# A graph layer on one core: two norms staggered in the last stage, one joint gather, and weights loaded during other stages

## What is computed

```python
K = typed_linear(x, Wk, bk, node_type)      # out[i] = x[i] @ W[type of i] + b[type of i]
Q = typed_linear(x, Wq, bq, node_type)
V = typed_linear(x, Wv, bv, node_type)
...                                         # attention over the edges, both ways; agg: [6250, 256]
h = jnp.concatenate([agg, agg], axis=1)
o = typed_linear(h, Wa, ba, node_type)      # Wa: [19, 512, 256]
y = o + x
mu = y.mean(axis=-1, keepdims=True)
var = y.var(axis=-1, keepdims=True)
yn = (y - mu) / jnp.sqrt(var + LN_EPS)
r = yn * gamma[node_type] + beta[node_type]
x = _layernorm(x + r, axis=-1)              # a second norm, over the sum with x
```

## Time and profile before

| | us |
|---|---|
| median of 3 runs (10157.53 to 10163.48) | 10160.39 |
| the profiled execution | 10144.25 |
| its span in the trace | 10142.5 |
| `project`: first load to PE's first product stage | 95.3 to 147.2 |
| `store_sums` and the loads of `output`: to PE's first transpose | 9388 to 9462.9 |
| the 18 turns of `output` and what follows them | 9462.9 to 10142.5 |

### The profile page before, as it was taken

How to read it: one execution, slowest core, us unless ns; L and a number is a source line. 1 busy time by engine, 2 the same in 40 slices (tenths; PEclk the granted TensorE clock), 3 DMA queues, 4 the chain that set the end, 5 groups by cost and what they waited for, 6 DMA issues and landing times. The chain is left out here.

```text
span 10142.5 us, 138050 instructions
## 1 busy us (share of the span) xinstructions
PE 6538.8 (64%) x34160; PEld 4384.0 (43%) x34161; DVE 6599.2 (65%) x13813; ACT 4385.9 (43%) x13293; POOL 5739.0 (57%) x5509
## 2 busy tenths in 40 slices
PE   3778666666664677777777677613666374998455
PEld 1257444444442444444444444402555263776222
DVE  1059999999996666666666666642555277888223
ACT  0100444444442555555555555412555274887111
POOL 3230677777776677777777777757888400000232
PEclk5665555555555888888888888756989797999555
DMA  2110000000001788888888888858999985887210
GB/s 67 46 53 0 9 9 9 9 9 9 9 9 42 246 262 262 261 260 261 258 260 260 258 260 260 230 182 272 336 332 336 194 199 166 258 259 225 94 35 12
DMA packets 1345184, 1653.53 MB, mean 163 GB/s; under 512 B 419468, under 2 KB 1144951, under 8 KB 1344777
## 3 DMA queue, kind: packets, MB, share of 16 engines
q1 hardware_dynamic: 868170, 967.89, 29.8%
q0 software_dynamic: 261440, 671.33, 22.0%
q10 hardware_dynamic: 215424, 12.91, 2.5%
HBM read 1047.72 MB, written 635.41 MB: 166 GB/s over the span
## 5 line engine op out<-in xcount | busy, mean ns | idle before, releaser
L1109 PE MATMUL exch_pG<-exch_tab,exch_ohT 128*128 x3328 | 1555.8, 625 | 930.9 <-ACT exch_kc L1031 926.1
L1532 PE MATMUL sum_pS<-sum_row,sum_oh 128*128 128x260 f32 x6656 | 1659.3, 406 | 700.3 <-issue 295.8
L976 POOL DMA_INDIRECT exch_row<-table,exch_of x1664 | 1677.2, 1008 | 555.8 <-issue 509.3
L821 POOL DMA_INDIRECT recs<-place_rec,place_addr x1568 | 1583.8, 1010 | 506.6 <-issue 483.0
L1532 PEld LDWEIGHTS sum_pS<-sum_row,sum_oh 128*128 128x128 f32 x6656 | 1297.9, 200 | 1061.4 <-issue 860.8
L1109 PEld LDWEIGHTS exch_pG<-exch_tab,exch_ohT 128*128 128x128 f32 x3328 | 781.2, 246 | 1690.0 <-issue 1505.4
L1571 DVE TENSOR_TENSOR sum_row<-sum_row,agg_al 128x1792 f32<-128x1792 f32 x416 | 841.1, 2022 | 504.9 <-DMA sum_row<-spill 491.7
L1190 POOL DMA_INDIRECT bys<-sum_pb x768 | 943.5, 1228 | 271.9 <-issue 224.1
L1190 POOL DMA_INDIRECT bys<-exch_pb x832 | 841.6, 1012 | 313.2 <-issue 247.9
L1554 ACT ACTIVATE sum_off<-kept_ramp,sum_neg 128x128 f32<-128x128 f32 x3328 | 1017.7, 388 | 0.0
L703 PE MATMUL place_pB<-place_rows,sort_sel 64*128 64x512 bf16 x784 | 464.6, 593 | 659.9 <-DVE place_junk L775 659.9
(11 more groups left out here) (298 smaller groups left out, 12452.7 us busy)
## 6 DMA issues: line engine op xcount, KB each, us to landing
spill<-exch_row SPq DMA_DIRECT2D x208, 1024.0 KB, 5.1
sum_row<-spill SPq DMA_DIRECT2D x208, 1024.0 KB, 7.7
sum_row<-bys SPq DMA_DIRECT2D x208, 1024.0 KB, 5.1
mid<-exch_pb SPq DMA_DIRECT2D x208, 528.0 KB, 4.6
sum_pb<-mid SPq DMA_DIRECT2D x192, 528.0 KB, 5.1
exch_row<-table,exch_of POOLq DMA_INDIRECT x1664
recs<-place_rec,place_addr POOLq DMA_INDIRECT x1568, 2.1
bys<-exch_pb POOLq DMA_INDIRECT x832, 3.5
```

The lines of the kernel that those rows point to most:

```text
L821: nc.gpsimd.indirect_dma_start(recs, bass.IndirectOffsetOnAxis(addr[:, par, 0, t:t + 1], 0), rec[:, par, t, :], None, bounds_check=last_sl ...
L976: nc.gpsimd.indirect_dma_start(row[q][:, t, TD:TD + S.TW], None, table, bass.IndirectOffsetOnAxis(of[q][:, t:t + 1], 0), bounds_check=last ...
L1109: nc.tensor.matmul(pG[t % 3][:, 0:VK], ohT[ring(j, 2)][:, t, :], flat[:, bass.ds(tiles[t] * GW, VK)], start=True, stop=True).then_inc(s_ga ...
L1532: last = nc.tensor.matmul(pS[h * HG + t // 2][:, 0:AW], oh[h][:, t, :], row[j][:, t, :], start=(t % 2 == 0), stop=(t % 2 == 1))
```

## The change

- **Weights of `project`.** ACT issues their nine loads in the block of `group_nodes`, into buffers that both stages share. The sums of weights on DVE stay in `project`.
- **One row for sums and x.** A new array `joint` in HBM has 512 columns. SP copies x into its right half during `project`, HBM to HBM; `store_sums` writes the sums into its left half.
- **Weights of `output`.** In the block of `store_sums` ACT issues four loads of `Wa`: two blocks into `W`, which lies in the place of the dead accumulator `k.acc0`, and two into a `W2` that holds both. DVE adds all of it in one instruction. A `Scope.retire` now stands ahead of `store_sums`.
- **gamma and beta.** SP loads them to all 128 partitions (`par`), 2 x 9.5 KB in each. The products into `pG` are gone.
- **Gathers.** One gather of 512 columns per tile takes the place of two of 256, straight by `k.nodes`; `idx` and ACT's copies are gone. There are three row buffers (`RB = 3`): the gathers of turn n wait for `z` of turn n - 3.
- **Two norms a turn apart.** DVE's and ACT's turn m does the first norm of turn m and the second norm of turn m - 1. One variance, one root and one reciprocal serve both. The row sums come out of the instructions that form `y` and `v` (`accum_out`) in place of L1757, and beta is added to x while ACT squares.
- **PE** has the transposes of turn n + 1 ahead of the products of turn n, and two sets of PSUM buffers.
- The loop is unrolled.

The diff, cut to its core:

```diff
@@ def projection_weights, called by ACT in group_nodes
+    for c in range(S.KC):
+        r = slice(c * P, (c + 1) * P)
+        nc.scalar.dma_start(w.Wqr[:, c, :, :], Wq[:, r, :].rearrange("t p n -> p t n")).then_inc(w.s_w, 16)
+        nc.scalar.dma_start(w.W[:, c, :, 0:S.PROJ], Wv[:, r, :].rearrange("t p n -> p t n")).then_inc(w.s_w, 16)
+        nc.scalar.dma_start(w.W[:, c, :, KO:S.TW], Wk[:, r, :].rearrange("t p n -> p t n")).then_inc(w.s_w, 16)
+    ...
@@ project, SP
-            for c in range(KC):
-                ...
+            sp.dma_start(joint[:, S.OUT:], x).then_inc(s_x, 16)
             for h in range(2):
                 sp.wait_ge(s_sc[h], 16 * B * (NBT // 2))
+            sp.wait_ge(s_x, 16)
@@ store_sums
+        @block.scalar
+        def _(act):
+            for c in range(OC):
+                nc.scalar.dma_start(W[:, c], Wa[:, c * P:(c + 1) * P, :].rearrange("t p n -> p t n")).then_inc(s_w, 16)
+                nc.scalar.dma_start(W2[:, c], Wa[:, OUT + c * P:OUT + (c + 1) * P, :].rearrange("t p n -> p t n")).then_inc(s_w, 16)
+        @block.vector
+        def _(dve):
+            dve.wait_ge(s_w, 32 * OC)
+            nc.vector.tensor_tensor(W, W, W2[:], ALU.add).then_inc(s_wr, 1)
@@ output, POOL
+            def gathers(n):
+                if n >= RB:
+                    pool.wait_ge(s_z, n - RB + 1)
+                    pool.sem_inc(s_turn, 1)
                 for j in range(B):
-                    for to, of in ((ag, sums), (xr, x)):
-                        ...
+                    nc.gpsimd.indirect_dma_start(row[n % RB][:, j, :], None, joint,
+                                                 bass.IndirectOffsetOnAxis(k.nodes[:, n * B + j:n * B + j + 1], 0),
+                                                 bounds_check=last_node, oob_is_err=False).then_inc(s_g[n % RB], 16)
+            ...
+            gathers(0)
+            gathers(1)
+            for n in range(NBT):
+                if n + 2 < NBT:
+                    gathers(n + 2)
                 pool.wait_ge(s_z, n + 1)
                 pool.sem_inc(s_turn, 1)
                 for j in range(B):
+                    nc.gpsimd.indirect_dma_start(out, bass.IndirectOffsetOnAxis(k.nodes[:, n * B + j:n * B + j + 1], 0), z[n % 2][:, j, :], None,
+                                                 bounds_check=last_node, oob_is_err=False).then_inc(s_sc[n % 2], 16)
@@ output, PE
+            def transposes(n):
+                h = n % 2
+                pe.wait_ge(s_g[n % RB], 16 * B * (n // RB + 1))
+                ...
+            transposes(0)
+            pe.wait_ge(s_b, 16)
+            for n in range(NBT):
+                if n + 1 < NBT:
+                    transposes(n + 1)
+                types = tile_types(nc, k, S, nc.tensor, n)
+                if n >= 2:
+                    pe.wait_ge(s_y, n - 1)
+                ...                                # products and biases of turn n
-                pe.wait_ge(s_gb, n)
-                for j in range(B):
-                    nc.tensor.matmul(pG[j][:].rearrange("p a n -> p (a n)"), k.ones[0:1, :], ...
@@ output, DVE
+            for m in range(NBT + 1):
+                n = m - 1
+                if n >= 0:
+                    nc.vector.tensor_scalar(mean[:, 1, :], total[:, 1, :], -1.0 / IN, None, ALU.mult).then_inc(s_m2, 1)
+                if m < NBT:
+                    types = tile_types(nc, k, S, nc.vector, m)
+                    x = row[m % RB][:, :, OUT:OUT + IN]
                     for j in range(B):
+                        dve.wait_ge(s_p, m * B + j // 2 * 2 + 2)
+                        last = nc.vector.scalar_tensor_tensor(out=y[:, j, :], in0=x[:, j, :], scalar=1.0, in1=pP[m % 2][j // 2][:, j % 2, :],
+                                                              op0=ALU.mult, op1=ALU.add, accum_out=total[:, 0, j:j + 1])
+                    ...                            # mean[:, 0]; x += beta; u = (y + mean) * gamma, each x4
+                    dve.wait_ge(s_q1, m + 1)
+                if n >= 0:
+                    dve.wait_ge(s_q2, n + 1)
+                nc.vector.tensor_scalar(var[:], dev[:], 1.0 / IN, LN_EPS, ALU.mult, ALU.add).then_inc(s_var, 1)
+                dve.wait_ge(s_root, m + 1)
+                link(nc.vector.reciprocal(inv[:], root[:]))
+                if n >= 0:
+                    ...
+                    for j in range(B):
+                        last = nc.vector.tensor_scalar(z[n % 2][:, j, :], v[:, j, :], mean[:, 1, j:j + 1], inv[:, 1, j:j + 1], ALU.add, ALU.mult)
+                    last.then_inc(s_z, 1)
+                    dve.wait_ge(s_z, n + 1)
+                if m < NBT:
+                    for j in range(B):
+                        last = nc.vector.scalar_tensor_tensor(out=v[:, j, :], in0=u[:, j, :], scalar=inv[:, 0, j:j + 1], in1=x[:, j, :],
+                                                              op0=ALU.mult, op1=ALU.add, accum_out=total[:, 1, j:j + 1])
```

More of the change, by code:

```diff
@@ L1628, in output @@
+def output(nc, k, S, W, joint, ba, gamma, beta, out):
+    T, OUT, IN, B, NBT, N, OC = S.T, S.OUT, S.IN, S.B, S.NBT, S.N, S.OC
+    RB = 3
     with ExitStack() as ctx:
         s = Scope(nc, ctx, "out")
-        W = s.sb("W", [P, OC, T, IN])
-        W2 = s.sb("W2", [P, T, IN])
-        bias = s.sb("bias", [1, T, 3 * IN])
-        idx = [s.sb(f"idx{h}", [P, B], I32) for h in range(2)]
-        xr = [s.sb(f"xr{h}", [P, B, IN]) for h in range(2)]
-        ag = [s.sb(f"ag{h}", [P, B, OUT]) for h in range(2)]
@@ L1647, in output @@
+        s_g = [s.sem(f"g{n}") for n in range(RB)]
         s_sc = [s.sem(f"sc{h}") for h in range(2)]
@@ L1862, in gnn_resnorm @@
                         aggregate(nc, k, S, Scope(nc, ctx5, "sum1"), 1, bys_v, 0, al, acc1)
[L1863 removed]
+                Scope.retire(nc)
+                W = k.acc0[:, 0:S.OC * S.T * S.IN].rearrange("p (c t n) -> p c t n", c=S.OC, t=S.T)
+                store_sums(nc, k, S, acc1, joint, W, Wa)
             Scope.retire(nc)
[L1865 to L1866 removed]
+            output(nc, k, S, W, joint, ba, gamma, beta, out)
+            Scope.retire(nc)
 _INS = ["x", "src", "dst", "edge_attr_5", "node_type_19", "L0_gnn_Wk", "L0_gnn_bk", "L0_gnn_Wq", "L0_gnn_bq", "L0_gnn_Wv",
```

238 lines of the change are left out of this document (105 added, 133 removed).

## The result

The changed kernel takes 9998.63 us (median of 4 runs, 9994.34 to 10001.43) beside 10160.78 us for the kernel before (4 runs). The ratio is 0.9836, 95% interval 0.9824 to 0.9847. The prediction was 9985 us, with a range of 9925 to 10045. The profiled execution has a span of 9992.6 us, 149.9 us less than the 10142.5 of the earlier trace rows.

The account below looks back on a forecast made before the run. The prediction took one serial loop through `z` to bound the last stage's turns: 9505.5 + 473 + 26 = 10004.5, with `project` minus 175.5 us in all; from the median 10160.4 that gives 9985 us, range 9925 to 10045.

Parts of the forecast that it names:

- The true pipeline: Rival for the last stage: gathers not late, PE bounds a turn at 14.7 us; 9733 us in all, chance 4%.
- The items of a turn: Six serial links of the last stage's loop from one `z` to the next, summed to 31.5 us.
- item 5: Last stage: PE's transposes and products until the last pair, put at 12.1 us, bounds 9.45 and 14.7.
- the sum over 15 turns: Last stage, from `z` of turn 0 to `z` of turn 15: the loop closes 15 times, 473 us.
- The passage: From `store_sums` to `output`: store and loads, 16.4 MB, take 55.5 us at 295 GB/s; overlap gains nothing.
- 37.5 us: Net saving in `project`: 39.5 us from weights loaded beside the grouping, less 2 us for the copy of x.
- late by as much as is gained: Rival at `project`: node types and grouping delayed by the weights, its gain lost; 10022 us, chance 3%.
- The unchanged stages: Stages between `project` and `store_sums`, whose code stays the same: no change in time, 0 us.
- The signs: Trace marks named beforehand, such as `project` transposes near 107.5 us and `z` every 29 to 34 us.
- the clock always up: Rival for the last stage: the clock rises in every turn, item 5 is 9.45 us; 9938 us, chance 17%.
- the clock never up: Rival for the last stage: the clock never rises, item 5 is 14.7 us; 10032 us, chance 22%.
- The slower side: Rival: moved HBM arrays slow unchanged stages, 1 us per `exchange` step, 208 us; 10193 us in all, chance 4%.

Follow-up runs that it names:

- e3: Changed kernel with PE's transposes of turn n + 1 behind the products of turn n; ratio to the kernel before 0.9746.
- e2: As e1, and the gathers wait for `v` instead of `z`, which comes one turn later; ratio to the kernel before 0.9655.
- e1: Changed kernel with POOL's gathers of turn n + 3 ahead of the scatters of turn n; ratio to the kernel before 0.9772.
- e9: Changed kernel with the loads of `Wa` and their sum in a block behind the store's; 9985.98 us, ratio to the kernel before 0.9827.
- e8: Changed kernel with ACT issuing the projection weights only after the node types have landed; ratio to the kernel before 0.9847.
- e10: e2 and e8 joined, gathers of turn n + 4 ahead of scatters of turn n, x copied behind `project`'s first turn; 9728.98 us, ratio to before 0.9576.
- e6: Kernel before with the array for the sums doubled, so that arrays behind it lie 6.4 MB further on; ratio to the kernel before 1.0007.
- e4: Changed kernel with every transpose of the last stage done twice, only the second pass waited for; ratio to the kernel before 0.9836.
- e7: Changed kernel with SP loading the projection weights in `project` again, the copy of x behind them; ratio to the kernel before 0.9877.

## Why the prediction was right

**The reading that decided** was that the last stage is no pipeline: POOL's and PE's queues close one loop through `z`. It held in every link, and three experiments moved it as the sums made from them say: the products (e3, 22.6 us against 22.9), the wait for `z` (e2, 34.1 us for two turns against 34), and the 5.2 us of scatters (e1; there the clock rose besides, 23.8 us against 28.8, and the last four turns, at the lower clock, fit the sum with 27.3). The true pipeline that the diff looks like needed another wait and another order.

**The items of a turn.** In the turn from 9521.49: `z` to POOL 0.85 (0.84), first scatter to last gather 9.16 (5.2 + 3.9), landing 3.71 (3.0), transposes to the second pair 14.31 (12.1), DVE to the end of `z` 6.06 (6.5). Together 34.1, where the forecast was 31.5 with bounds of 28.9 and 34.2. Two terms were mis-sized. The landing was 0.7 us longer. And item 5 was a mix where the clock took one side: I chose the middle since one row with transposes ahead pointed up and those without pointed down; in ten of the first eleven turns it stayed down. By these turns alone this made 10 x 2.2 us too little.

**What made up for it** I did not see: the last four turns take 27.4 to 27.6 us. The landing there is 2.15 us, since little is left in their tiles to gather (14 GB/s in the stretch, against 41), and in these turns the clock rises (0.64). Why it does is not shown: in the last four turns of e1, with less idle time still, it does not. So the sum over 15 turns was off by 5.4 us, by two errors of opposite sign; the term was right by luck as much as by working.

**The passage** was 8.5 us shorter. The wrong step is "At 295 this is 55.5 us": 16.4 MB took 47 us at 349 GB/s. The rates of the earlier trace rows, at DMA shares of 0.83 and 0.88, are means over stretches with idle edges in them, and I read them as the rates of engines nearly full. In the same trace of the kernel before the store moves 351 to 355 GB/s once it runs (9390 to 9406 us) and the loads 347 to 371 (9414 to 9438). The Trainium skill, "DMA: Bandwidth & Descriptors", section "Issuing engines are not separate DMA queues", has it that a second issuing engine saves only issuing time. By that rule the overlap buys next to nothing, and the traces come close to it: e9 measured 4.8 us, about the length of the idle gap between its two blocks. (`par` is 2 x 19 KB in each partition, two DMAs of 2432 KB, and not 2 x 9.5; the 5 MB of the prediction are right.)

**`project`** gave 29.0 and not 37.5 us. The rival "late by as much as is gained" was right in kind and small in size: the block began 6.3 us late, for the most part because the node types shared the DMA engines with 11 MB that ACT had issued beside them. I had counted the 49 scatters of the grouping, and not the one small load at its head that everything waits for. e8 shows it for 5 us of the 6.3. From the block's start to PE's transposes another 3 us were lost, by which the first gathers came late: two of them stretched (last section), and I had put the copy of x at 2 us. It lengthens their landing: from the last one's start to PE's transposes 5.4 us with the copy beside it (111.40 to 116.78), 2.85 without it in e10 (105.32 to 108.17).

**The unchanged stages** were forecast at nothing and took 19.5 us more in the trace, the largest error of the sum, and unexplained. In the medians it is less, since the profiled execution of kernel before lay 16 us under its median and that of the changed one 4. That is how a sum that missed by 25.6 us missed the median by 13.6.

**The signs.** POOL's eight indirect DMAs in a row, the transposes released by the DMA of `out_row` and the span of `exchange` (7 us apart) came as said. PE's transposes in `project` at 107.5 (116.78) and the end of the long sum at 9417.6 (9436.34) did not, and the last four turns lie below the 29 to 34 us.

The rivals: the clock always up and the clock never up were both wrong, and the truth lies nearer to the second. The slower side is excluded by e6 as far as 0.3%.

## What to carry to other kernels

Buffers make a pipeline only if the order of every queue lets them: write the loop down from one signal to the same signal one turn on, with each engine's queue order as a link, and count the turns it spans. Here one wait on an earlier signal and the gathers ahead of the scatters took the last stage from 555 to 310 us (e10), more than the whole change gained. When loads are moved under other work, ask which small load that work starts with, and put the large ones behind it. And price PE's work behind a wait at both levels of the clock, and let rows decide between them: here one stage of the same run stood at 0.94 and another at 0.56.

## What the runs showed of the hardware

**More work on PE made the turn shorter.** 16 more transposes a turn, 1.7 us of work, took it from 34.0 to 30.8 us (e4). I had thought of the clock as a property of the stage; it can differ from turn to turn (28.7 us beside 34.0 in one stage).

**POOL's gathers stretch beside DVE's sums.** In the changed kernel the first two gathers of `project` took 2.92 and 2.09 us, in e7, where DVE is idle then, 1.05 and 1.01. It is not the copy of x, which e10 does not have there:

```profile
98.02 2.38 DVE L364 TENSOR_TENSOR weights_W<-weights_W,weights_Wqr 128x2128 f32<-128x2128 f32 x1
98.40 2.92 POOL L333 DMA_INDIRECT proj_xr<-in_x,proj_idx  x1 [0.93 <-POOL proj_xr L345]
100.43 1.11 DVE L365 TENSOR_TENSOR weights_W<-weights_W,weights_Wqr 128x912 f32<-128x912 f32 x1
101.57 1.25 DVE L363 TENSOR_TENSOR weights_bias<-weights_bqr 1x1064 f32<-1x1064 f32 x1
101.62 2.09 POOL L333 DMA_INDIRECT proj_xr<-in_x,proj_idx  x1 [0.31 <-issue]
```

Each gather starts within a sum of two SBUF operands and ends about 0.9 us after the sum. The Trainium skill, "SBUF — State Buffer", section "SBUF: two separate sides", says that a DVE operation with two SBUF inputs and a GpSimd operation that reads SBUF exclude one another for the whole instruction. The rows agree for a gather that starts within a long sum, and it cost 3 us at the head of the stage. They do not show the other direction: the sum at 100.43 runs its 1.11 us, as in the kernel before, while the first gather is still under way. And in the last stage the scatter at 9523.72 takes 1.03 us beside DVE's `v`, which reads two operands in SBUF in instructions of 0.48 us. Memsets on POOL beside the same sums kept their 0.95 us.

**A small load beside large ones.** The node types (24 KB) landed some 5 us later beside 11 MB issued by another engine (DVE's start at 12.04 and 6.97 us, e8).
